# The scan's DRAM buffers with the images innermost: one load of records per chunk, and larger loads and stores around it

## The reference, cut to what matters

```python
xn = layernorm(x as [4, 4096, 512])
XQ, XK = rope(xn @ q_w.T), rope(xn @ k_w.T);  XV = xn @ v_w.T       # per head
eta = token_idx * sigmoid(xn . lr_w + lr_b) / 64                    # per token and head
for chunk of 16 tokens:                    # 256 of them, in order, per image and head
    Z1   = xk @ W + b
    grad = d/dZ of the layernorm loss(Z1, target xv - xk)
    out  = xq + ln(xq @ W - (eta * tril(xq xk^T)) @ grad + b - tril(eta) @ grad)
    W   -= (eta_last * xk)^T @ grad;   b -= sum(eta_last * grad)
y = layernorm(out) @ o_w.T
```

## Time and profile before

| | us |
|---|---|
| median of 3 runs (lowest to highest) | 6241.13 (6234.36 to 6241.5) |
| profiled execution's own time | 6242.9 |
| its span, first to last instruction | 6241.0 |
| projection, from about 215 to 1645 | 1430 |
| scan and read, from the first chunk at 1716.6 | to 4411 |
| drain of the tiles within it, after the last chunk at 4335 | 76 |
| spectral layers and gating behind it | to 6241 |

### The profile page before, as it was taken

One profiled execution on the slowest core, in us unless ns is written; L12 is line 12 of the kernel. 1 busy time (PEld: TensorE's weight loads), 2 busy tenths in 40 slices (PEclk: granted clock), 3 DMA queues, 4 the chain that ended last, 5 costly groups with the idle time before them and its releaser, 6 DMA issues. The chain is left out here.

```text
span 6241.0 us, 144090 instructions
## 1 busy us (share of the span) xinstructions
PE 5393.6 (86%) x42556; PEld 3821.0 (61%) x42556; DVE 3919.7 (63%) x14026; ACT 2368.3 (38%) x6675; POOL 2385.5 (38%) x3910
## 2 busy tenths in 40 slices
PE   1799999999588888888888888888799999599999
PEld 0344444444267777777777777777666666377777
DVE  5566666666377777777767777777566666544444
ACT  0111111111055555555555555555333333233333
POOL 0244444444255455555545554454122222122222
PEclk9899999999779899989999998999899999799999
DMA  6233333333344444444444444444212221222221
GB/s 246 72 128 120 127 120 127 120 128 120 127 106 119 125 119 123 118 122 118 119 119 121 120 120 120 118 122 126 98 77 87 87 87 45 78 88 87 87 87 70
DMA packets 823279, 693.73 MB, mean 111 GB/s; under 512 B 357224, under 2 KB 758000, under 8 KB 811664
## 3 DMA queue, kind: packets, MB, share of 16 engines
q1 hardware_dynamic: 732304, 542.54, 29.1%
q10 hardware_dynamic: 90240, 142.75, 6.1%
HBM read 402.96 MB, written 282.20 MB: 110 GB/s over the span
## 5 line engine op out<-in xcount | busy, mean ns | idle before, releaser
L1390 PE MATMUL proj_ps<-proj_w_sb,proj_h 128*128 128x512 f32 x3072 | 1345.6, 596 | 0.0
L1390 PEld LDWEIGHTS proj_ps<-proj_w_sb,proj_h 128*128 128x128 f32 x3072 | 577.2, 190 | 743.4 <-issue 716.6
L2195 PE MATMUL scan_ps_y<-scan_o_t,proj_wo_sb 128*128 128x128 f32 x4096 | 648.2, 307 | 2.1 <-ACT scan_o_t L1827 2.1
L1312 DVE SCALAR_TENSOR_TENSOR proj_lin<-proj_ps,proj_rstd,proj_wbias_sb 128x512 f32<-128x512 f32 x384 | 284.5, 748 | 545.8 <-PE proj_ps L1390 544.8
L2195 PEld LDWEIGHTS scan_ps_y<-scan_o_t,proj_wo_sb 128*128 128x128 f32 x4096 | 565.1, 214 | 50.8 <-issue 8.6
L1737 POOL TENSOR_TENSOR scan_b_step<-scan_core,scan_rate_last 128x128 f32<-128x128 f32 x512 | 318.6, 622 | 650.5 <-DVE scan_core L1984 650.5
L1963 DVE TENSOR_TENSOR scan_zg<-scan_ps_z,scan_gain 128x128 f32<-128x128 f32 x512 | 146.1, 285 | 563.1 <-ACT scan_square L1798 518.0
L1798 ACT ACTIVATE scan_square<-scan_ps_z 128x64 f32<-128x64 f32 x1024 | 218.6, 220 | 651.0 <-PE scan_ps_z L2113 645.4
L1791 ACT COPY scan_state_w<-scan_ps_w 128x512 f32<-128x512 f32 x480 | 281.3, 586 | 476.1 <-PE scan_ps_w L2125 455.5
L2125 PE MATMUL scan_ps_w<-scan_step,scan_record 64*128 64x128 f32 x4088 | 386.5, 312 | 12.4 <-DVE scan_step L1989 11.9
L1266 POOL TENSOR_TENSOR proj_gk<-proj_rec,proj_gain_sb 128x256 f32<-128x256 f32 x256 | 181.5, 729 | 554.5 <-DVE proj_rec L1333 554.5
(11 more groups left out here) (290 smaller groups left out, 12327.7 us busy)
## 6 DMA issues: line engine op xcount, KB each, us to landing
scan_record<-records SPq DMA_DIRECT2D x1032, 98.0 KB
records<-proj_rec ACTq DMA_DIRECT2D x128, 784.0 KB, 3.6
scan_k_in<-records SPq DMA_DIRECT2D x266, 128.0 KB
spectra<-fourier_spec SPq DMA_DIRECT2D x16, 2112.0 KB, 6.4
fourier_spec<-spectra SPq DMA_DIRECT2D x16, 2112.0 KB, 8.2
stats_x<-x SPq DMA_DIRECT2D x16, 2048.0 KB, 7.7
proj_h<-x SPq DMA_DIRECT2D x32, 1024.0 KB, 7.1
queries<-proj_q ACTq DMA_DIRECT2D x128, 256.0 KB, 3.7
```

What stands on the lines that cost most here:

```text
L1312: v.scalar_tensor_tensor(lin[q][:, n], ps[q][n][:], rstd[k][:, j:j + 1], T.wbias[:, n], ALU.mult, ALU.add).then_inc(lin_sb.sem, 1)
L1390: last = pe.matmul(ps[j % 2][n][:], h[k][:, ct, j * P:(j + 1) * P], T.w[:, n, ct], start=ct == 0, stop=ct == CT - 1)
L2195: pe.matmul(ps_y[:, n], T.wo[:, ct, n * P:(n + 1) * P], o_t[:, ct], start=ct == 0, stop=False)
```

## The change

The images become the innermost dimension but one of the DRAM buffers that the scan reads and writes: `records` is [head pair][token][parity][image][196], `gradients` [head pair][token][parity][image][64], and the snapshots [superchunk][group][128][2 images][64]. `queries` keeps its layout. With that:

- the records of a chunk come in one load for all images (128 rows of 3136 bytes) into one buffer of a ring of 4, and both groups wait for the same load; the gradients leave in one store per group (128 rows of 512 bytes), the snapshots in one per group;
- the projection stores the records of a sub-step in two DMAs, one per parity (512 rows of 784 bytes each), and issues its eight stores of zeros ahead of its loop, behind the first `normalise`, and no longer behind it;
- queries, x and the output move per superchunk, 1 MB each, with SBUF buffers for 4 images, two of each: queries in chunk 3 for use from the next superchunk's chunk 1 on, x of the superchunk before in chunk 1, the output of the one before that in chunk 7;
- the gradients of a tile are read in two loads, one per parity (512 rows of 256 bytes each); the bias rows and the keys in the same number and size of pieces as before, from other strides;
- what only the projection needs in SBUF is freed behind it.

```diff
@@ project, ScalarE
-                    act.dma_start(rec[bass.ds(b, 1), :, bass.ds(g * 512 + j * P, P)].rearrange("o a t n e -> (o t) a (n e)"),
-                                  rec_sb[:, j].rearrange("p (a n) e -> p a (n e)", n=2)).then_inc(rec_out[j].sem, 16)
+                    for n in range(2):
+                        act.dma_start(rec[:, bass.ds(g * 512 + j * P, P), n, bass.ds(b, 1)].rearrange("a t o e -> (o t) a e"),
+                                      rec_sb[:, j].rearrange("p (a n) e -> p a n e", n=2)[:, :, n]).then_inc(rec_out[j].sem, 16)
...
             normalise(0, 0, 0)
+            act.wait_ge(init.sem, init.at(0, 1))
+            for a in range(NH // 2):
+                for n in range(2):
+                    act.dma_start(rec[a, TOK + n * P:TOK + (n + 1) * P].rearrange("t n b e -> t (n b e)"), zero[:]).then_inc(pad_out.sem, 16)
             rows_out(0)
...
             loop(act, body)
-            act.wait_ge(init.sem, init.at(0, 1))
-            for b in range(B):
-                for n in range(2):
-                    act.dma_start(rec[b, :, TOK + n * P:TOK + (n + 1) * P].rearrange("a t n e -> t a (n e)"), zero[:]).then_inc(pad_out.sem, 16)
@@ scan_and_read, SyncE
-            def load_record(g, ring, s):
-                for b in range(PB):
-                    sp.dma_start(record[g][ring][:, b, :], rec[PB * g + b, :, bass.ds(s * CS, CS)].rearrange("a t n e -> a (t n) e")
-                                 ).then_inc(rec_in[g][ring].sem, 16)
+            def load_record(ring, s):
+                sp.dma_start(record[ring][:].rearrange("p b e -> p (b e)"), rec[:, bass.ds(s * CS, CS)].rearrange("a t n b e -> a (t n) (b e)")
+                             ).then_inc(rec_in[ring].sem, 16)
...
                     if c == 0:
                         for g in range(GR):
                             sp.wait_ge(b_sum_sb[g].sem, b_sum_sb[g].at(s, 0))
-                            for b in range(PB):
-                                sp.dma_start(s_snap[bass.ds(((v * 2 + at.p) * B + PB * g + b) * P, P), :],
-                                             b_sum[g][0][:, b, :]).then_inc(snap_gone[g].sem, 16)
+                            sp.dma_start(s_snap[bass.ds(v * 2 + p, 1), g].rearrange("o p b e -> (o p) (b e)"),
+                                         b_sum[g][0][:].rearrange("p b e -> p (b e)")).then_inc(snap_gone[g].sem, 16)
                     for g in range(GR):
                         sp.wait_ge(state_ps[g].sem, state_ps[g].at(s, -1))
-                        load_record(g, (c + 2) % RING, s + 2)
-                if at.odd:
-                    ...
-                        sp.wait_ge(y_done.sem, y_done.at(t, 1))
-                        sp.dma_start(o_view[b, :, :, bass.ds(sc * P, P)], y_sb[b % 2][:]).then_inc(y_gone[b % 2].sem, 16)
-                    ...
-                        sp.dma_start(x_sb[b % 2][:], x_view[b, :, :, bass.ds(sc * P, P)]).then_inc(x_loaded[b % 2].sem, 16)
+                    load_record((c + 2) % RING, s + 2)
+                if c == 1 and (scan or p == 0) and (not isinstance(v, int) or v * 2 + p):
+                    sp.dma_start(x_sb[1 - p][:], x_view[:, :, bass.ds((v * 2 + p - 1) * P, P)]).then_inc(x_loaded[1 - p].sem, 16)
                 if scan:
                     for g in range(GR):
                         sp.wait_ge(stored_sb[g].sem, stored_sb[g].at(s, 1))
-                        for b in range(PB):
-                            sp.dma_start(grad[PB * g + b, :, bass.ds(s * CS, CS)].rearrange("a t n e -> a (t n) e"),
-                                         stored[g][c % 2][:, b, :]).then_inc(grad_gone[g][c % 2].sem, 16)
+                        sp.dma_start(grad[:, bass.ds(s * CS, CS), :, PB * g:PB * g + PB].rearrange("a t n b e -> a (t n) b e"),
+                                     stored[g][c % 2][:]).then_inc(grad_gone[g][c % 2].sem, 16)
+                if c == 7 and (not isinstance(v, int) or v):
+                    sp.wait_ge(y_done.sem, y_done.at(v * 8 + p * 4 - 4, 0))
+                    sp.dma_start(o_view[:, :, bass.ds((v * 2 + p - 2) * P, P)], y_sb[p][:]).then_inc(y_gone[p].sem, 16)
...
-                        sp.dma_start(grad_sb[q][:].rearrange("p (a n) e -> p a (n e)", n=2),
-                                     grad[b, :, bass.ds(sc * P, P)].rearrange("a t n e -> t a (n e)")).then_inc(grad_in[q].sem, 16)
                         for n in range(2):
+                            sp.dma_start(grad_sb[q][:].rearrange("p (a n) e -> p a n e", n=2)[:, :, n],
+                                         grad[:, bass.ds(sc * P, P), n, b].rearrange("a t e -> t a e")).then_inc(grad_in[q].sem, 16)
...
-                    tile = at.tile(KQ - 1)
-                    ...
-                        sp.wait_ge(qb_sb.sem, qb_sb.at(t, -1))
-                        load_query(t, b, sc)
+                elif scan:
+                    if c == 3:
+                        if not isinstance(v, int):
+                            sp.wait_ge(qb_sb.sem, qb_sb.at(v * 8 + p * 4 - 4, 0))
+                        sp.dma_start(q_sb[p][:].rearrange("p b h e -> p b (h e)"), q_in[:, bass.ds((v * 2 + p) * P, P)].rearrange("b n c -> n b c")
+                                     ).then_inc(q_loaded[p].sem, 16)
@@ network
-    rec = dram("records", (B, NH // 2, TOK + 2 * P, 2, RW))
+    rec = dram("records", (NH // 2, TOK + 2 * P, 2, B, RW))
-    grad = dram("gradients", (B, NH // 2, TOK, 2, HD))
-    s_snap = dram("sum_snapshots", (TOK // P * B * P, HD))
+    grad = dram("gradients", (NH // 2, TOK, 2, B, HD))
+    s_snap = dram("sum_snapshots", (TOK // P, 2, P, B // 2, HD))
```

More of the change, by code:

```diff
@@ L1432, in each @@
             return [sb(f"{n}{g}", shape) for g in range(GR)]
-        record = many("record", [P, PB, RW], RING)
+        record = [sb(f"record{q}", [P, B, RW]) for q in range(RING)]
         stored = many("stored", [P, PB, HD], 2)
@@ L1649, in body @@
             def body(at, scan):
[L1650 removed]
+                s, c, v, p = at.s, at.c, at.v, at.p
                 if scan:
@@ L1681, in body @@
                     if tile:
-                        t, b, sc, _ = tile
+                        t, b, sc, par, half = tile
                         g, q = b // PB, b % 2
@@ L2146, in tile_weighted @@
             def tile_weighted(tile):
-                t, b, sc, par = tile
+                t, b, sc, par, half = tile
                 for n in range(2):
```

141 lines of the change are left out of this document (63 added, 78 removed).

## The result

| | before | after |
|---|---|---|
| median us (lowest to highest, 4 runs each) | 6241.3 (6234.4 to 6241.8) | 6126.9 (6118.4 to 6138.9) |
| profiled execution's own time | 6242.9 | 6138.9 |
| scan, mean of 14 loop iterations, us | 166.6 | 160.6 |
| SyncE in the middle of the scan, waits in 1000 us | 0.3 | 9.1 |

The ratio is 0.982, with an interval of 0.980 to 0.984: faster by 114 us (1.8%), where 309 were forecast. The sign is right, the size is not, and 6127 lies above the range's upper end of 6090.

A forecast was written before the change was run, and what follows sets the result against it. SyncE's issues or the four DMA engines carrying records bound the scan; the change relieves both. Gains: 288 us scan iterations + 6 first iteration + 16 projection end - 1 start = 309, so 5932 us, range 5850 to 6090.

The forecast's parts named there:

- the DMA side after the change: Scan, DMA work per chunk: records 4.4, gradients 1.7, the rest 2.7, in all 8.8 us, up to 9.7 corrected.
- All others: Scan DMAs besides records and gradients: 672 KB per chunk at 269 GB/s, 2.5 us, plus 0.2 for smaller gradient reads.
- compute mean of 8.96: Scan, compute time per chunk: floor of 137.4 us plus 6 us for the loop's branch, over 16 chunks.
- 4 us of near-tie: Scan: waiting added per iteration because DMA and compute rates are so near, 4 us, with ends 0 and 10.
- SyncE itself falls out of the race: Scan: SyncE's issues per two chunks drop to 13.25 from 25 and take 8 to 11 us of 18.
- A: Scan: the four engines stay the bound, 9.6 us a chunk, 154 us an iteration, 6031 us; chance 0.22.
- C: Scan: 1 MB transfers delay records, gradient and key loads; at full length 374 us lost, 6305 us; chance 0.05.
- B: Scan: nothing of DMA is left and the branch costs less, 141 us an iteration, 5835 us; chance 0.14.
- The price of a late load: Scan: TensorE's wait of 4.84 us for queries costs a chunk 7.6 us, as the clock is low after it.
- The branch: Scan, loop's branch back: costs 6 us per iteration, with bounds of 2 and 10.
- The first iteration: Scan's first loop iteration, which holds few tiles: gains 6 us (0 to 20).
- The projection: Zero padding leaves the projection's end, gaining 16 us; its eight issues at the start cost 1 us.

The follow-up runs named there:

- records by ACT: Changed kernel with only the scan's record loads issued by ACT at the start of each chunk, in place of SyncE: 6092.2 us, ratio 0.975.
- records per image: Changed kernel with only its record load cut into four DMAs, one per image, of 784-byte rows: 6038.7 us, ratio 0.966.
- no 1 MB transfers: Changed kernel with x, queries and y moved per image in the odd chunks, in place of 1 MB per superchunk: 6034.6 us, ratio 0.967.
- both: Changed kernel with record loads cut into four, one per image, and x, queries and y moved per image in the odd chunks: 6002.6 us, ratio 0.960.
- two engines: Changed kernel with its record load cut into two DMAs of two head pairs each: 6996.0 us, ratio 1.119.
- records wide: Changed kernel with its record load cut into four, one per head pair, of 32 rows of 3136 bytes: 5813.7 us, ratio 0.931.
- narrow records with wide gradients: Changed kernel with only its gradient stores cut into four each, one per head pair, 8 per chunk in place of 2: 6165.8 us, ratio 0.987.
- wide gradients on top of wide records: Changed kernel with its record load and its two gradient stores each cut into four DMAs, one per head pair: 6177.7 us, ratio 0.989.

## Why the prediction was wrong

**What set the pace.** The table puts the load of the four engines beside the mean chunk of each kernel. Records are 401 KB by 89 GB/s for rows of 784 bytes (between the 87 and 92 of the earlier trace rows), by 91 for rows of 3136 and by 50 on two engines, from the windows above. Gradients are 2.0 us before the change; with two stores per chunk a window of the changed kernel with nothing else in flight gives 78 GB/s for 131 KB, 1.7 us:

```profile
1711.40:1712.10 0.70, 0.20 (x8) 0.00 (x0) 0.57 (x2) 0.43 (x4) 0.31 (x1) 0.50 0.27 78
```

The rest is what the mean DMA share from 2000 to 3600 us leaves, spread over 16 engines. For the changed kernel: 0.50 x 16 x 10.04 = 80.3 engine-us per chunk, less 4.4 x 0.26 x 16 = 18.3 and 1.7 x 0.27 x 16 = 7.3, leaves 54.7, or 3.4 us on each.

| kernel | share | records + gradients + rest | mean chunk |
|---|---|---|---|
| before | 0.45 | 4.5 + 2.0 + 2.9 = 9.4 | 10.41 |
| changed | 0.50 | 4.4 + 1.7 + 3.4 = 9.5 | 10.04 |
| records by ACT | 0.49 | 4.4 + 1.7 + 3.2 = 9.3 | 9.87 |
| records per image | 0.48 | 4.5 + 1.7 + 3.0 = 9.2 | 9.65 |
| no 1 MB transfers | 0.49 | 4.4 + 1.7 + 3.1 = 9.2 | 9.58 |
| both | 0.49 | 4.5 + 1.7 + 3.0 = 9.2 | 9.47 |
| two engines | 0.34 | 8.0 + 1.7 + 3.1 = 12.8 | 13.39 |
| records wide | 0.56 | 0 + 1.7 + 4.4 = 6.1 | 8.71 |

Every kernel with narrow records is somewhat above its sum, and the kernel that nearly doubles the record term on two engines moves by it: 13.4 - 10.0 = 3.4 of 3.6. The one that takes it away falls to compute, 8.6 by the earlier trace rows. The sums are estimates, and low ones: their terms are those of DMAs that run alone. Among other transfers the same packets take longer. The queue row of the run with ACT gives the records 12.7% of 16 engines, which on four is 51% of the 9.87 us, 5.0 and not 4.4; with it that kernel's sum is 9.8, its mean chunk. Counted by packet size, the records of the changed kernel take 5.5. No sum is better than half a us.

Two things the table does not settle. The kernel before is 1.0 above its sum, with 12.5 issues per chunk on a SyncE that waits for nothing either; no run separates the two there. And narrow records with wide gradients have 4.4 + 3.9 = 8.3 at a mean chunk of 10.2: SyncE's time, held issues included, is what is left to explain it.

Point by point:
- **The step that failed** is the DMA side after the change, 8.8 us a chunk as the sum of 4.4 + 1.7 + 2.7. Its record and gradient terms are right for DMAs alone (91 and 78 GB/s). "All others", taken at the 269 GB/s of the earlier trace rows, are 3.4 and not 2.7: with the x load in flight all engines together moved 199 GB/s, a record load included. And in company the records take 5.0 or more. The sum is 9.5 from the windows and about 10 with 5.0 for records. The prediction's upper end of 9.7 was too low by its own rule: the fifth that takes 9.0 to 10.7 in the kernel before takes 8.8 to 10.5. At 8.8 the sum lay below the compute mean of 8.96, at 9.5 and more above it, and that decides who waits.
- **The 4 us of near-tie** then had to be a bound, not a near-tie: 9.5 x 16 = 152 and not 147.4. The 8.6 us from there to the measured 160.6 are mostly what the change itself brought in by single record loads and 1 MB bursts: with both undone the iteration is 151.5.
- **"SyncE itself falls out of the race"** was wrong as stated. The 8 to 11 us of 18 would hold for its issues at their shortest (some 300 us in 1000); in fact they take 807, most of it held, and SyncE shows no slack. The run with ACT, where SyncE waits a third of the time for a gain of 35 us, speaks for this being more an effect of the full engines than a cause.
- **The rivals.** A, "the four engines stay the bound", is what happened in kind and should have been the forecast; it had 0.22. Its numbers were for the changed kernel, which took 160.6 and not 154, 6127 us and not 6031. That the kernels with one of the two kinds of unevenness undone measured just that (154.3 and 153.3, 6039 and 6035) is in part luck. C, bursts in front of records, is real but worth 92 us, not 374; it turned no gain into a loss. Its condition, a lead of two chunks or 17 us for a record, was not met: SyncE runs behind, and the median lead was 8.0 us. B, compute only, is what wide records reach: 139.4 against 141, 5814 against 5835.
- **The price of a late load.** Right in kind: the wait of 4.9 us in the chunk of 17.37 cost 8.35, at a clock of 0.70.
- **The branch**, taken at 6 us an iteration, is 139.4 - 137.4 = 2.0 where no load is late. That term was too dear by 4, and it hid in part what the DMA term lacked.
- **The first iteration** did not gain 6 but lost 3.5. With wide records it took 123.5 (1701.54 to 1825.05) in place of 131.5, so narrow records cost there too.
- **The projection**: 16.9 measured for 16. At its start the eight issues took 8.4 us and cost nothing. The copy that reads the row sums came 0.6 us later than in the earlier trace rows, but so did ACT's first normalise, ahead of the issues (before, then changed):

```profile
203.94 2.92 ACT L1181 ACTIVATE proj_h<-proj_h,proj_gn_now 128x512 f32<-128x512 f32 x4 [8.36 <-DMA proj_rope<-rope]
```

```profile
204.57 0.81 ACT L1181 ACTIVATE proj_h<-proj_h,proj_gn_now 128x512 f32<-128x512 f32 x1 [8.55 <-DMA proj_rope<-rope]
...
207.92 5.20 ACTq L1231 DMA_DIRECT2D records<-proj_zero  x4
213.29 0.59 ACT L1188 COPY proj_st_rows<-proj_ps_rows 128x512 f32<-128x512 f32 x1 [5.79 <-PE proj_ps_rows L1363]
```

**Still open**: what the limit is at which an issue is held; what set the pace of narrow records with wide gradients; and why one record load is worse than four with the same bytes on the same engines. That the engines run dry while SyncE issues and are then late in one piece would fit, but no run here separates it.

## What to carry to other kernels

Before merging DMAs, read from the windows on how many engines each runs, and add up the time of the busiest engine, the wide transfers' share in it too; if that sum is near the stage's pace, fewer or longer DMAs gain little, and taking the outermost small dimension out of the access pattern does more: here that one edit gave 313 us on top of the change's 114. Rates read from windows with one DMA alone make the sum too low. Mind the number of issues too: wide gradients on top of wide records took it all back. A queue that waits for nothing is not thereby the bound: compare each issue's median with its shortest, and where they differ look at what the issue stands behind. When a kernel is short of an engine, removing the largest wait can just hand the lateness to the next load in the order: 195 us of waits gone were worth 28.

## What was not expected of the hardware

- A narrow DMA (outer dimension 4) took SyncE 0.54 to 0.62 us to issue at the shortest, the others 0.31 to 0.43, whatever their bytes: the record load of 392 KB 0.618, gradient stores 0.552 narrow and 0.314 wide, bias rows of 16 KB 0.328, the x load of 1 MB 0.391.
- Issues in the changed kernel are held up to 8.9 us, the longest behind 1 MB loads, and this shows in no wait. On ACT's queue, with records alone, none took over 0.62 us in the same stretch in which SyncE's were held up to 8.5.
- Rows four times as long (3136 for 784 bytes) gave 91 GB/s for 87 to 92 at a DMA share of 0.26 to 0.28.
- At a share of 0.13, two engines, records moved at 50 GB/s, at 0.26, four engines, at 91: 25 and 23 each.
